# Region attention on one core: two regions share their scores, attend and turn runs, and VectorE takes over the turned reciprocals

## What is computed

```python
q_r = pool(q) ...                      # mean over each region
a_r = q_r @ k_r                        # 49 x 49 affinities per image
_, idx_r = jax.lax.top_k(a_r, TOPK)    # TOPK = 4
attn = softmax(einsum('bhnqd,bhnkd->bhnqk', qs * SCALE, key_g))
out = einsum('bhnqk,bhnkd->bhnqd', attn, val_g)
out = out + lepe                       # 3x3 depthwise convolution of v, plus bias
out = einsum('nchw,oc->nohw', out, out_w) + out_b
x = x + out
```

## Time and profile before

| what | value |
|---|---|
| median of 3 runs | 1749.04 us (1747.19 to 1750.9) |
| the profiled execution | span 1746.7 us |
| instructions | 76311 |
| PE busy | 1689.8 us |
| ACT busy | 1463.2 us |
| DVE busy | 1527.7 us |
| POOL busy | 1169.5 us |
| granted TensorE clock, mean | 0.999 of full speed (2.4 GHz) |

### The profile page before, as it was taken

One profiled execution on the slowest core, in us unless ns is written; L12 is line 12 of the kernel. 1 busy time (PEld: TensorE's weight loads), 2 busy tenths in 40 slices (PEclk: granted clock), 3 DMA queues, 4 the chain that ended last, 5 costly groups with the idle time before them and its releaser, 6 DMA issues.

```text
span 1746.7 us, 76311 instructions
## 1 busy us (share of the span) xinstructions
PE 1689.8 (97%) x26568; PEld 1365.2 (78%) x26568; DVE 1527.7 (87%) x3327; ACT 1463.2 (84%) x4793; POOL 1169.5 (67%) x2548
## 2 busy tenths in 40 slices
PE   4999999999999999999999999999999999999997
PEld 4878887877878878778778778787777887777775
DVE  6588989898998999998898998989998888899994
ACT  2488888898888888888888888888888888887875
POOL 3266666677666776776767776667766666677873
PEclk9999999999999999999999999999999999999999
DMA  5234434343434443443444443434443334466664
GB/s 201 77 96 124 131 110 139 114 148 115 137 117 133 118 145 118 124 131 118 133 130 126 126 135 116 139 109 142 125 125 102 111 106 127 134 194 202 218 208 165
DMA packets 164649, 234.61 MB, mean 134 GB/s; under 512 B 19232, under 2 KB 146912, under 8 KB 164272
## 3 DMA queue, kind: packets, MB, share of 16 engines
q1 hardware_dynamic: 141408, 129.71, 25.6%
q0 software_dynamic: 22864, 100.02, 17.3%
...
## 4 chain that ended last, share of the span: by engine, by line
PE 62%; ACT 18%; DVE 13%; issue 4%; DMA 1%; POOL 0%; SPq 0%; ACTq 0%; POOLq 0%; DVEq 0%
PE chunk_bank L1026 17%; ACT probs L622 14%; PE pt_bank L1126 13%; PE s_bank L1113 13%; PE o_bank L1140 8%; DVE neg_max L852 6%; PE chunk_bank L1040 6%; DVE lepe L742 5%; PE chunk_bank L1068 2%; ACT probs_t L629 2%; PE o_bank L1150 1%; PE s_bank L1026 1%; ACT v_stage L594 1%; PE chunk_bank L1088 1%; DMA xn<-x_dram 1%
## 5 line engine op out<-in xcount | busy, mean ns | idle before, releaser
L622 ACT ACTIVATE probs<-s_bank,neg_max 128x256 f32<-128x256 f32 x1568 | 739.6, 484 | 154.8 <-DVE neg_max L852 154.5
L852 DVE TENSOR_REDUCE neg_max<-s_bank 128x2 f32<-128x512 f32 x784 | 506.2, 686 | 129.4 <-PE s_bank L1113 127.8
L742 DVE SCALAR_TENSOR_TENSOR lepe<-v_band,taps,lepe 128x448 f32<-128x448 f32 x896 | 611.3, 728 | 0.0
L386 POOL COPY k_sel<-k_all 128x128 f32 x1568 | 419.4, 311 | 269.2 <-PE s_bank L1113 257.8
L1026 PE MATMUL chunk_bank<-xn,wqkv 128*128 128x224 f32 x2544 | 568.7, 355 | 2.5 <-DVE xn L778 2.5
L629 ACT COPY probs_t<-pt_bank 128x512 f32<-128x512 f32 x784 | 467.3, 596 | 60.3 <-PE pt_bank L1126 58.9
L1126 PE MATMUL pt_bank<-ident,probs 128*128 128x128 f32 x3136 | 492.5, 280 | 0.2
L1026 PEld LDWEIGHTS chunk_bank<-xn,wqkv 128*128 128x128 f32 x2544 | 440.8, 192 | 8.7 <-DVE xn L778 2.6
L1126 PEld LDWEIGHTS pt_bank<-ident,probs 128*128 128x128 f32 x3136 | 358.5, 141 | 53.0 <-ACT probs_t L629 0.9
L397 POOL TENSOR_TENSOR lepe<-o_norm,lepe 128x128 f32<-128x128 f32 x392 | 248.2, 633 | 154.5 <-DVE o_norm L870 153.3
L622 ACT ACTIVATION_READ_ACCUMULATOR probs<-s_bank,neg_max 128x1 f32 x1568 | 332.4, 212 | 0.0
...
## 6 DMA issues: line engine op xcount, KB each, us to landing
...
```

The costliest lines, as they stand in the source:

```text
L386: last = pool.tensor_copy(k_sel[:, r % K_SLOTS, :, RT * j:RT * (j + 1)], k_all[:, b % 2, :, bass.ds(reg[j] * RT, RT)])
L622: act.activation(probs[:, u, :], s_bank[:, u, 0:KEYS], ACT.Exp, bias=neg_max[:, r % 2, u:u + 1], accum_out=denom[:, r % 2, u:u + 1]).then_ ...
L742: ins = dve.scalar_tensor_tensor(row, v_band[:, n % BANDS, k, t // 3:t // 3 + RS, t % 3:t % 3 + W], taps[:, k, t:t + 1], row, ALU.mult, AL ...
L852: dve.tensor_reduce(neg_max[:, r % 2, 2 * hf:2 * hf + 2], s_bank[:, 2 * hf:2 * hf + 2, 0:KEYS], AX.X, ALU.max, negate=True).then_inc(max_d ...
```

## The change

Regions are grouped in pairs (`DUOS`), with one region of each image alone (the first one; in the last image the last one). `BODIES` lists for each pair the slots that it carries, the two slots one before its regions; projections stay as they were per slot, in `early_part` and `late_part`.
- The scores of both regions run one behind the other, in the two halves of the four banks; then both attends of the pair before; then its two turned reciprocals.
- A turn now holds one head position of both regions, so a pair has four turns. `probs` keeps four blocks, used by turns alternately. PE runs in a body: scores, attends of the pair before, its reciprocals, early part of the first slot, turn 0, late part, turn 1, early part of the second slot, turn 2, late part, turn 3.
- ACT runs in a body: evacuations of the first slot, copy of turn 3 of the pair before, exponentials of turn 0 and 1, copy of turn 0, evacuations of the second slot, exponentials of turn 2, copy of turn 1, exponentials of turn 3, copy of turn 2. `recips_out` is gone.
- DVE runs in a body: reciprocal and spread of the pair before (straight into `o_norm`), four maxima, then a copy of the turned reciprocals out of `o_bank` into `o_norm` and the multiply in place, then the taps and the rest of both slots. Statistics of an image are regrouped.
- `side` moves to the first columns of `o_bank`, with waits on `o_normed` before its users. `v_sel` has four slots, `idx_row` has one. POOL gathers the next pair's keys at the start of a body and adds both regions of the pair before at its second slot.

The core of the diff:

```diff
-V_SLOTS = 3
+V_SLOTS = 4
...
+def duos():
+
+
+    for b in range(NB):
+        alone = 0 if b < NB - 1 else NREG - 1
+        i = 0
+        while i < NREG:
+            n = 1 if i == alone else DUO
+            yield b * NREG + i, n
+            i += n
+
+
+DUOS = list(duos())
+DUO_OF = {first + i: h for h, (first, n) in enumerate(DUOS) for i in range(n)}
+BODIES = [(h, [first + i - 1 for i in range(n) if first + i]) for h, (first, n) in enumerate(DUOS)]
+BODIES += [(len(DUOS), [ALL - 1, ALL]), (len(DUOS) + 1, list(range(ALL + 1, STEPS * NWIN)))]
...
-        probs_t = sb("probs_t", [P, 2, 2, 2 * CH * P])
+        probs_t = sb("probs_t", [P, HG, 2 * CH * P])
         k_sel = sb("k_sel", [P, K_SLOTS, KC, KEYS])
         v_sel = sb("v_sel", [P, V_SLOTS, CH, C])
-        o_norm = sb("o_norm", [P, 2, P])
-        recips = sb("recips", [P, HG, HD])
-        recips_t = sb("recips_t", [P, P])
-        neg_max = sb("neg_max", [P, 2, HG])
-        denom = sb("denom", [P, 2, HG])
-        rdenom = sb("rdenom", [P, 2, HG])
+        o_norm = sb("o_norm", [P, DUO, P])
+        neg_max = sb("neg_max", [P, 2, DUO * HG])
+        denom = sb("denom", [P, 2, DUO * HG])
+        rdenom = sb("rdenom", [P, 2, DUO * HG])
...
-            return s_bank[:, HG - 1, KEYS + at:KEYS + at + n]
+            return o_bank[:, at:at + n]
...
+            for h, slots in BODIES:
+                for r in regions_of(h + 1):
+                    gather_keys(r)
+                for i, slot in enumerate(slots):
+                    s, rc = divmod(slot, NWIN)
+                    rr, kv, xr = s % NWIN, s + KV_LEAD, s + STAT_LEAD
+                    if i == min(1, len(slots) - 1):
+                        for r in regions_of(h - 1):
+                            take_region(r)
...
+            def exp(h, j):
+                if not is_duo(h):
+                    return
+                t = turns_before(h) + j
+                act.wait_ge(max_done, t + 1)
+                if t >= 2:
+                    act.wait_ge(probs_turned, t - 1)
+                if j == 0 and h >= 2:
+                    act.wait_ge(inv_done, h - 1)
+                for i, (u, at) in enumerate(heads_of(h, j)):
+                    col = 2 * j + i
+                    act.activation(probs[:, 2 * (j % 2) + i, :], s_bank[:, u, KEYS * at:KEYS * (at + 1)], ACT.Exp,
+                                   bias=neg_max[:, h % 2, col:col + 1],
+                                   accum_out=denom[:, h % 2, col:col + 1]).then_inc(exp_done, 1)
+
+            def probs_t_out(h, j):
+                if not is_duo(h):
+                    return
+                act.wait_ge(probs_turned, turns_before(h) + j + 1)
+                if j == 0 and h:
+                    act.wait_ge(attn_done, DUOS[h][0])
+                act.copy(probs_t[:, j, :], pt_bank[:, :]).then_inc(probs_t_evac, 1)
...
+            exp(0, 0)
+            q_out(1, 0)
+            exp(0, 1)
+            probs_t_out(0, 0)
+            q_out(1, 1)
+
+            for h, slots in BODIES[1:]:
+                if slots:
+                    chunk_out(slots[0])
+                if is_duo(h - 1):
+                    probs_t_out(h - 1, turns_of(h - 1) - 1)
+                exp(h, 0)
+                exp(h, 1)
+                probs_t_out(h, 0)
+                for slot in slots[1:]:
+                    chunk_out(slot)
+                if is_duo(h) and turns_of(h) == 2 * DUO:
+                    exp(h, 2)
+                    probs_t_out(h, 1)
+                    exp(h, 3)
+                    probs_t_out(h, 2)
...
+            def maximum(h, j):
+                first, n = DUOS[h]
+                dve.wait_ge(scores_done, first + n)
+                scored = (s_bank[:, j, 0:n * KEYS].rearrange("p (i c) -> p i c", i=n) if n == DUO
+                          else s_bank[:, 2 * j:2 * j + 2, 0:KEYS])
+                dve.tensor_reduce(neg_max[:, h % 2, 2 * j:2 * j + 2], scored, AX.X, ALU.max, negate=True
+                                  ).then_inc(max_done, 1)
+
+            def invert(h):
+                first, n = DUOS[h]
+                dve.wait_ge(exp_done, HG * (first + n))
+                dve.reciprocal(rdenom[:, h % 2, 0:n * HG], denom[:, h % 2, 0:n * HG]).then_inc(inv_done, 1)
+
+            def spread(h):
+                n = DUOS[h][1]
+                dve.wait_ge(inv_done, h + 1)
+                if h:
+                    dve.wait_ge(o_row_done, DUOS[h][0])
+                dve.tensor_copy(o_norm[:, 0:n, :].rearrange("p i (u d) -> p i u d", u=HG),
+                                rdenom[:, h % 2, 0:n * HG].rearrange("p (u i) -> p i u", i=n).unsqueeze(3)
+                                .to_broadcast([P, n, HG, HD])).then_inc(recips_done, 1)
+
+            def normalize_o(h):
+                n = DUOS[h][1]
+                o = o_norm[:, 0:n, :].rearrange("p i c -> p (i c)")
+                dve.wait_ge(recips_turned, h + 1)
+                dve.tensor_copy(o, o_bank[:, DUO * P:(DUO + n) * P]).then_inc(recips_evac, 1)
+                dve.wait_ge(recips_evac, h + 1)
+                dve.tensor_tensor(o, o_bank[:, 0:n * P], o, ALU.mult).then_inc(o_normed, 1)
...
+            for h, slots in BODIES[1:]:
+                if is_duo(h - 1):
+                    invert(h - 1)
+                    spread(h - 1)
+                if is_duo(h):
+                    for j in range(turns_of(h)):
+                        maximum(h, j)
+                if is_duo(h - 1):
+                    normalize_o(h - 1)
+
+                for slot in slots:
...
+            def scores(h):
+                if not is_duo(h):
+                    return
+                first, n = DUOS[h]
+                if h:
+                    pe.wait_ge(exp_done, HG * first)
+                for i in range(n):
+                    r = first + i
+                    g, rc = divmod(r, NWIN)
+                    pe.wait_ge(k_sel_done, r + 1)
+                    if rc == 0:
+                        wait_taken(pe, "q", g, 0)
+                        wait_taken(pe, "q", g, 1)
+                    if r == 0:
+                        for bank in (2, 3, 4):
+                            pe.wait_ge(chunk_free[bank], early_chunks[bank])
+                    for u in range(HG):
+                        s = slice(HD * u, HD * (u + 1))
+                        for k in range(KC):
+                            last = pe.matmul(s_bank[RT * k:RT * (k + 1), u, KEYS * i:KEYS * (i + 1)],
+                                             q_all[s, g % Q_RING, k, rc, :], k_sel[s, r % K_SLOTS, k, :],
+                                             start=True, stop=True)
+                    last.then_inc(scores_done, 1)
+
+            def turn_probs(h, j):
+                if not is_duo(h):
+                    return
+                t = turns_before(h) + j
+                if t:
+                    pe.wait_ge(probs_t_evac, t)
                 else:
                     pe.wait_ge(chunk_free[5], early_chunks[5])
-                pe.wait_ge(exp_done, HG * r + 2 * hf + 2)
-                for u in (2 * hf, 2 * hf + 1):
+                pe.wait_ge(exp_done, 2 * (t + 1))
+                for i in range(2):
                     for c in range(CH):
-                        at = P * (CH * (u % 2) + c)
-                        t = pe.transpose(pt_bank[:, at:at + P], probs[:, u, P * c:P * (c + 1)], ident[:])
-                t.then_inc(probs_turned, 1)
-
-            def attend(r):
-                pe.wait_ge(v_sel_in[r % V_SLOTS], 16 * TOPK * (r // V_SLOTS + 1))
-                pe.wait_ge(recips_evac, r + 1)
-                if r:
-                    pe.wait_ge(o_normed, r)
-                pe.wait_ge(probs_t_evac, 2 * r + 2)
-                for k in range(KC):
-                    for c in range(CH):
-                        for u in range(HG):
-                            head = HG * k + u
-                            at = P * (CH * (u % 2) + c) + RT * k
-                            last = pe.matmul(o_bank[HD * u:HD * (u + 1), RT * k:RT * (k + 1)],
-                                             v_sel[:, r % V_SLOTS, c, HD * head:HD * (head + 1)],
-                                             probs_t[:, r % 2, u // 2, at:at + RT],
-                                             start=(c == 0), stop=(c == CH - 1))
-                last.then_inc(attn_done, 1)
-
-            def turn_recips(r):
-                pe.wait_ge(recips_done, r + 1)
-                if r:
-                    pe.wait_ge(o_normed, r)
-                pe.transpose(o_bank[:, P:2 * P], recips[:].rearrange("p u d -> p (u d)"),
-                             ident[:]).then_inc(recips_turned, 1)
+                        at = P * (CH * i + c)
+                        ins = pe.transpose(pt_bank[:, at:at + P], probs[:, 2 * (j % 2) + i, P * c:P * (c + 1)],
+                                           ident[:])
+                ins.then_inc(probs_turned, 1)
+
+            def attend(h):
+                first, n = DUOS[h]
+                if h:
```

(41 more changed lines are left out.)

535 lines of the change are left out of this document (233 added, 302 removed).

## The result

The changed kernel takes 1864.87 us (median of 4 runs, 1859.38 to 1868.12) against 1748.32 beside it: 1.0664 times the time before, interval 1.0641 to 1.0687. The forecast was slower, at 1813, and its range ended at 1850: the direction came out, the size did not. The profiled span is 1864.6 where the sum gave 1810.7, so 53.9 us are missing from it. The granted clock was 0.997 of full, 0.999 before: both at the 2.4 GHz level.

A forecast was written before the change was run, and what follows sets the result against it. Bound before: TensorE's work and the ring, nearly equal; with pairs, a longer ring of 8.38 us plus waits inside the body. Steps summed to +64, span 1810.7, median 2.3 above: 1813 us; range 1725 to 1850.

The forecast's parts named there:

- the ring: Scores, maxima, exponentials, then next scores, which wait for the last exponential: 3.99 us for a region before the change.
- part 2: Path from a pair's scores through ScalarE's exponentials and copies to turn 3: no pair under 8.38 us, 7.88 without evacuation.
- part 4: VectorE, GpSimd, transfers: hidden while a pair takes longer; VectorE 0.1 us more a pair, ScalarE's spared copies buy nothing.
- part 3: TensorE and ScalarE waiting for each other inside the body: mean extra 0.51 us in full rows, 0.27 in short rows.
- What bounds now: Kernel before: TensorE's work and the ring, coupled, within 0.25 us of each other; the longer decides.
- Part 1: TensorE's scores, attends and turns get shorter by 0.36 us a pair, 70 us if TensorE stays the bound.
- the first rival: TensorE stays the bound, its 70 us come out and waits are cut too: 1679; chance 0.14.
- The second: The ring holds but waits inside the body are absorbed, pairs 8.38 everywhere, 7.95 in the tail: 1735; chance 0.12.
- The third: TensorE changes shape as often as before inside the longer runs, 35 us more: 1847; chance 0.04.
- The fourth: VectorE becomes a bound of its own, pairs 9.1 us on average, 73 us more: 1885; chance 0.06.
- The sum: Full steps +33.4 us, short +17.0, first and last +14.6, tail -1: +64, span 1810.7.

The follow-up runs named there:

- the first experiment: Changed kernel with the early part of the first slot placed between a pair's scores and the attends of the pair before; 1883.43 us, ratio 1.076.

## Why the prediction was right and wrong

The direction and the ring of part 2 were right. What failed: no term for how fast TensorE's instructions arrive, 24.9 us of the missing 54; part 4's "hidden" for VectorE, which costs 0.61 to 0.69 in (4,5) and 0.87 in single regions; and the extras of part 3 in short rows, full rows and the tail. Without the first alone the time would have been near 1840 (an estimate, 1864.9 less 24.9), inside the range.

- **What bounds now**, two coupled engines: right. Taking a quarter off ScalarE's exponentials moved the kernel before by 1.1% only, since TensorE at 97% stood right behind.
- **Part 1, TensorE's savings**: scores 1.05 (1.15 forecast), attend 1.04 (1.04), reciprocals 0.27 (0.27). The savings came out and bought nothing: the 148.8 us of the earlier trace rows fell to 96.3, of which 16.5 are standstills, and beside them stand 234.9 of turns waiting for copies. The rule of the Trainium skill (TensorEngine Tiling (Array Packing), Key Properties) that a change of mode drains the engine agrees with the 0.17 of the additional change in the first experiment; it named a true cost, and the first rival built on it fell because that cost wasn't on the longer of the two paths.
- **Part 2, a floor of 8.38**: 8.33 measured, in pairs (2,3), and its reading holds too. Timeline of such a body, changed kernel, scores, ScalarE and the last turn:

```profile
226.68 1.12 PE L1175 MATMUL s_bank<-k_sel,q_all 32*64 32x256 f32 x32
...
228.63 0.47 ACT L671 ACTIVATE probs<-s_bank,neg_max 128x256 f32<-128x256 f32 x1 [1.26 <-DVE neg_max L905]
...
230.46 0.59 ACT L681 COPY probs_t<-pt_bank 128x512 f32<-128x512 f32 x1
...
232.37 0.60 ACT L681 COPY probs_t<-pt_bank 128x512 f32<-128x512 f32 x1
...
233.75 0.63 ACT L681 COPY probs_t<-pt_bank 128x512 f32<-128x512 f32 x1
...
234.43 0.66 PE L1192 MATMUL pt_bank<-ident,probs 128*128 128x128 f32 x4
235.01 1.12 PE L1175 MATMUL s_bank<-k_sel,q_all 32*64 32x256 f32 x32
```

  From the first exponential to copy 2 ScalarE doesn't pause. What the part didn't see is how close the other path is: TensorE's turn 0 at +3.12 allows copy 0 0.64 later, at +3.76; ScalarE is ready for it at +3.78. So half the exponentials won 0.2 to 0.3 there and not 0.9. "What saved scores latency once a pair was given away to a third copy, the evacuation and turn 3" fits: putting turn 3 behind the next scores returned 0.22 a pair against the first experiment.
- **Part 3, extras by slot pair**: six of seven kinds of full pair within 0.07. The step that failed is (4,5), 0.61 too small in 14 bodies: 8.5 us. In short rows I said "only (4,5), (5,6), (6,0) remain, mean 0.27", but short rows never hold (5,6), and (0,1) and (2,3) there wait 0.29 and 0.23 for an evacuation that hangs on the late part, as I had seen for (6,0) alone: some 8 us with the last rows. For full rows I averaged all seven kinds (0.51), but 21 of the 23 have only (1,2), (3,4) and (5,6), whose own extras average 0.62 (measured 0.60): 5.5 us too little. First rows were 5 us too much. That these two nearly cancel is luck.
- **Part 4, what is covered**: for VectorE it took 0.1 and called it hidden. It priced the three large operations (296, 410 and 419 ns; 1.13 together, forecast 1.2) rightly and their order wrongly. They stand ahead of the taps and the emptying of the output's bank, and the bank is what TensorE waits for in (4,5). In a body with a single region (timeline of the changed kernel, its scores and VectorE) the order bites again:

```profile
528.76 0.69 PE L1175 MATMUL s_bank<-k_sel,q_all 32*64 32x256 f32 x16
...
529.89 0.19 DVE L911 RECIPROCAL rdenom<-denom 128x8 f32<-128x8 f32 x1
...
530.11 0.39 DVE L918 COPY o_norm<-rdenom 128x256 f32<-128x256 f32 x1
...
530.42 1.27 DVE L905 TENSOR_REDUCE neg_max<-s_bank 128x2 f32<-128x512 f32 x2
```

  Scores of this body start at 528.76, so maxima could start near 529.55; VectorE is late by 0.87, and the body takes 5.43 instead of 4.55. With six of them 5 us. The tail's bodies with an evacuation of q add about 6 beyond the forecast. Of ScalarE's spared copies it said "this buys nothing": 9 us. For GpSimd and the transfers of values no row of TensorE's waits has more than 3 us, and for the side results none that wasn't there before (19.5 us in the opening, before 19.9).
- **The term that was missing altogether**: TensorE's standstills without a semaphore, 24.9 us, which make up most of the 30 above the medians. No attend of before shows one above 0.4. There scores and attend are 48 passes and as many loads; a pair issues 96 and 96 in 2.1 us. Their cause is the fetch of instructions, as the place in the block and the landings show; the prediction never asked what could grow with the length of a run.
- **The rivals**: the first (1679) had TensorE as bound; half the attends left (2,3) where it was. The second (1735) had the extras absorbed; they aren't. The third (1847), no saving, is nearest in time and falls by 1.05 and 1.04. The fourth (1885) is nearly as near and wrong in cause: VectorE is at 82% and waits 237.4 us for scores.
- **The sum**: +64 forecast, +118 by the spans. About 24 us are mis-sized pairs and 30 are bodies above their median. The range covered errors of the terms that the sum had, and left nothing for one that it lacked.
